# A macaron block on one core: order of two weight loads, of a root and of two kinds of parts

## The reference

```python
x = x + 0.5 * ffn(layernorm(x))
x = x + mamba2_mixer(layernorm(x))
x = x + 0.5 * ffn(layernorm(x))
```

## Time and profile before

| what | value |
| --- | --- |
| median of 3 runs | 1654.56 us |
| the runs | 1654.16, 1654.56, 1661.31 us |
| the profiled execution: its own time | 1658.09 us |
| its span, first to last instruction | 1656.2 us |
| TensorE (PE) busy | 1621.9 us, 98% of the span |
| VectorE (DVE), ScalarE (ACT), GpSimd (POOL) busy | 1033.3, 626.5, 377.0 us |
| mean granted clock of TensorE | 0.999 |

### The profile page before, as it was taken

One profiled execution on the slowest core, in us unless ns is written; L12 is line 12 of the kernel. 1 busy time (PEld: TensorE's weight loads), 2 busy tenths in 40 slices (PEclk: granted clock), 3 DMA queues, 4 the chain that ended last, 5 costly groups with the idle time before them and its releaser, 6 DMA issues.

```text
span 1656.2 us, 25046 instructions
## 1 busy us (share of the span) xinstructions
PE 1621.9 (98%) x9672; PEld 1311.9 (79%) x9672; DVE 1033.3 (62%) x2022; ACT 626.5 (38%) x934; POOL 377.0 (23%) x298
## 2 busy tenths in 40 slices
PE   6999999989999999999999999999999999999999
PEld 3788788867888778888877888877888877888887
DVE  6444345766676877777786677777675683543333
ACT  4334334454333464333355334256333341122111
POOL 1655662012222212222122122122122121000000
PEclk9999999999999999999999999999999999999999
DMA  9755654744455354444435445545544447556763
GB/s 286 293 190 208 224 196 165 254 167 157 155 157 167 130 176 148 158 161 151 163 119 174 165 150 166 162 135 184 165 155 156 155 128 217 166 178 187 219 199 131
DMA packets 253427, 290.46 MB, mean 175 GB/s; under 512 B 14464, under 2 KB 211200, under 8 KB 244096
## 3 DMA queue, kind: packets, MB, share of 16 engines
q1 hardware_dynamic: 253312, 288.88, 53.4%
HBM read 238.51 MB, written 50.33 MB: 174 GB/s over the span
## 4 chain that ended last, share of the span: by engine, by line
PE 72%; DVE 4%; ACT 2%; issue 1%; DMA 0%; SPq 0%; ACTq 0%; DVEq 0%
PE bank L1184 30%; PE bank L1225 14%; PE bank L1140 12%; PE bank L1253 5%; PE bank L1322 3%; PE bank L1293 2%; PE bank L1309 2%; PE bank L1271 2%; PE bank L1316 1%; PE bank L1281 1%; DVE xT L1740 0%; DVE m_cv L1781 0%; DVE res L1766 0%; PE bank L1168 0%; PE bank L1150 0%
## 5 line engine op out<-in xcount | busy, mean ns | idle before, releaser
L1184 PE MATMUL bank<-fxT,wj 128*128 128x512 f32 x1752 | 415.3, 390 | 1.2 <-DVE xn L1753 1.2
L1184 PEld LDWEIGHTS bank<-fxT,wj 128*128 128x128 f32 x1752 | 328.7, 188 | 70.1 <-DVE xn L1753 1.7
L1225 PE MATMUL bank<-m_wd,m_hb 128*128 128x512 f32 x1128 | 278.8, 393 | 1.9 <-DVE m_hb L1759 1.9
L1225 PEld LDWEIGHTS bank<-m_wd,m_hb 128*128 128x128 f32 x1128 | 209.1, 188 | 47.3 <-issue 5.0
L1535 ACT CAST m_hb<-xn 128x512 fp32r<-128x512 f32 x96 | 59.5, 620 | 455.1 <-DVE xn L1753 455.1
L1140 PE MATMUL bank<-xT,wi 128*128 128x512 f32 x900 | 222.6, 395 | 1.6 <-DVE m_cv L1781 0.5
L1140 PEld LDWEIGHTS bank<-xT,wi 128*128 128x128 f32 x900 | 166.1, 188 | 39.1 <-issue 4.5
L1766 DVE TENSOR_TENSOR res<-bank,res 128x512 f32<-128x512 f32 x192 | 132.5, 690 | 83.4 <-PE bank L1225 81.2
L2084 POOL TENSOR_TENSOR m_L<-m_L,m_GT 128x512 f32<-128x512 f32 x36 | 52.6, 1461 | 436.0 <-ACT m_L L1544 436.0
L1753 DVE SCALAR_TENSOR_TENSOR xn<-bank,sc,xn 128x512 f32<-128x512 f32 x96 | 71.8, 748 | 123.0 <-PE bank L1184 122.9
L1529 ACT ACTIVATE xn<-bank,sc 128x512 f32<-128x512 f32 x96 | 66.1, 688 | 145.8 <-PE bank L1184 140.3
(11 more groups left out here) (222 smaller groups left out, 2312.4 us busy)
## 6 DMA issues: line engine op xcount, KB each, us to landing
wj<-ug_split SPq DMA_DIRECT2D x167, 512.0 KB, 4.2
m_wd<-dn_split SPq DMA_DIRECT2D x48, 1024.0 KB, 4.8
wi<-in_split SPq DMA_DIRECT2D x76, 512.0 KB, 3.3
ug_split<-b_wu SPq DMA_DIRECT2D x8, 2048.0 KB, 14.1
m_wo<-out_split SPq DMA_DIRECT2D x32, 512.0 KB, 4.1
wi<-ug_split SPq DMA_DIRECT2D x25, 512.0 KB, 4.1
in_split<-b_msp SPq DMA_DIRECT2D x20, 512.0 KB, 3.7
raw<-in_wug SPq DMA_DIRECT2D x8, 1024.0 KB, 7.0
```

The costliest lines, as they stand in the source:

```text
L1184: ins = pe.matmul(to[:], w[:, a, k, :], frm[:, b, k, :], start=(k == 0 and i == 0), stop=(k == KH - 1 and i == 2))
L1225: ins = pe.matmul(F[t % 2][:], hb[:, a, j, ck(t)], wd[:, b, j, :], start=(j == 0 and n == 0), stop=(j == 1 and n == 2))
```

## The change

Three places are changed.

- In the second stage SyncE issues `load_up(131)` and `load_up(132)` ahead of `load_down(32)`, where they came right behind it. For items 0 to 2 nothing moves there.
- For the sixth item's statistics VectorE runs the second `next` in block b = 4 and the third with `bias` in b = 5; both and `bias` were in b = 4. On ScalarE the four `beside_row`s of b = 5 move behind `hidden_high(37, 1)` and `silu(38, 0)`.
- In the first stage ScalarE casts the parts for the next unit's turns (`high_half`) ahead of the unit's two mixer blocks (`high_blocks`), and GpSimd subtracts in the same order (`low_half` ahead of `low_block`).

No instruction is added or removed.

```diff
--- before.py
+++ after.py
@@ -441,11 +441,11 @@
                 for g in range(2):
                     if g and c + 2 < NC:
                         butterflies(c + 2, True)
+                    for key in halves_of(2 * c + g + 1):
+                        low_half(key)
                     if c:
                         low_block(4 * (c - 1) + 2 * g)
                         low_block(4 * (c - 1) + 2 * g + 1)
-                    for key in halves_of(2 * c + g + 1):
-                        low_half(key)
 
         @block.tensor
         def _(pe):
@@ -688,9 +688,9 @@
                     hidden_high(n, j)
                 for key in keys[3]:
                     turn(key)
-                high_blocks(n)
                 for key in halves_of(n + 1):
                     high_half(key)
+                high_blocks(n)
             silu(UNITS - 1, 0)
             silu(UNITS - 1, 1)
             high_blocks(UNITS - 1)
@@ -1086,6 +1086,9 @@
                         load_out(last_pair(q, b) + 1)
                     if not end:
                         load_up(4 * at + 7)
+                if q == BATCH - 1:
+                    load_up(4 * NC * BATCH + 3)
+                    load_up(4 * NC * BATCH + 4)
                 if other:
                     load_down(NC * (q + 1))
                 if more:
@@ -1094,10 +1097,8 @@
                     keep(q + 1)
                     heads(q + 1, 0)
                     load_in(m0 + 2 * NB + 6)
-                if mix:
+                if more:
                     load_up(4 * NC * (q + 1) + 3)
-                if q == BATCH - 1:
-                    load_up(4 * NC * BATCH + 4)
                 if q >= 2:
                     g = beside(q)
                     for t in range(TPG):
@@ -1713,12 +1714,12 @@
                 if at == NC * BATCH:
                     square(q - 1, NB - 1)
                 silu(at, 1)
+                hidden_high(at, 1)
+                if at < NC * ITEMS - 1:
+                    silu(at + 1, 0)
                 if q == BATCH and b == 5:
                     for t in range(TPG):
                         beside_row(q + 1, t)
-                hidden_high(at, 1)
-                if at < NC * ITEMS - 1:
-                    silu(at + 1, 0)
                 if q == BATCH and b == 6:
                     for t in range(TPG):
                         beside_turn(q + 1, t)
@@ -2047,10 +2048,9 @@
                     norm(q - 1)
                 if q == BATCH and b == 2:
                     ending(q - 1)
-                if q == BATCH and b in (3, 4):
+                if q == BATCH and b in (3, 4, 5):
                     next(other)
-                if q == BATCH and b == 4:
-                    next(other)
+                if q == BATCH and b == 5:
                     bias(1, s_fs)
                 hidden(at, 1)
                 if pair >= 0:
```

## The result

The changed kernel takes 1651.62 us in the median of 20 runs (1648.65 to 1656.31), the kernel before 1656.89 us, also in 20 runs (1654.03 to 1661.31), the three of the table above among them. The ratio is 0.9967 with a 95% interval of 0.9960 to 0.9974, so the change gains 5.5 us of 1656.9, between 4.3 and 6.6. The forecast was 4.83 us, and 1649.7 us against a median of before that stood at 1654.56 then. The profiled execution has a span of 1652.4 us, 3.8 less than before.

The account below looks back on a forecast made before the run. TensorE's stream was taken to bound the kernel, so only its waits count: 2.58 + 1.65 + 0.60 = 4.83 us, taking the median from 1654.56 to 1649.7 us, range 1645.5 to 1657.

Parts of the forecast that it names:

- The bound: Whole kernel: TensorE busy 1621.9 us of a 1656.2 us span; only its waits, 34.3 us idle in all, can be saved.
- The rival that nothing arrives at the end: Whole kernel: a later point is not bound by TensorE's stream, so no gain, 1654.6 us; chance 0.07.
- First stage, 2.58 us: First stage: with parts ahead of blocks, four late pairs of units return to 35.78 us; gain 2.58 us, bounds 0 and 2.6.
- The count of the block loads' delay: First stage: loads into `mraw` land 3.7 us later, ScalarE's `silu` comes 1.3 us late, cost to TensorE 0.
- The cover: First stage: the bank is free at about 207.2, TensorE's third turn needs it at 209.8, so 2.6 us are left.
- the first stage's count: First stage: fetched weights come at 192.3 instead of 188.6, butterflies end at 197.1, GpSimd's next parts covered by about 1 us.
- Fifth item, 1.65 us: Second stage, fifth item: loads ahead of the down load remove the wait before `up1(32)`; gain 1.65 us, bounds 0 and 1.7.
- Sixth item, 0.60 us: Second stage, blocks 4 and 5: root over three blocks removes `down`'s wait for VectorE's hidden value; gain 0.60 us, bounds 0.47 and 0.7.
- The step on ScalarE's rows: Sixth item: four rows, 2.92 us, move behind `silu(38, 0)`; unmoved they would stand before a cast that `down(37)` needs.
- The sum: Whole kernel: 2.58 + 1.65 + 0.60 = 4.83 us, median from 1654.56 to 1649.7 us, 0.29% less.
- One of its own signs of being wrong: Whole kernel: prediction wrong if the three gains are there and the span is not 4 to 5 us shorter.
- The rival on the slower side: First stage: late block loads hold ScalarE, TensorE waits 3.7 us in each of four units, 1667.1 us; chance 0.04.

## Why the prediction was right

- **The bound.** TensorE's stream sets the time from the first stage to the end; its busy time stayed within 0.2 us (1624.4 us in the second profile of the changed kernel, where the clock fell for longer) and what was removed are waits. The rival that nothing arrives at the end is refuted by the ratio.
- **First stage, 2.58 us.** 2.54 in the changed kernel's profile, 2.55 in the profile and 2.2 (0.7 to 3.5) by time with this part alone. The count of the block loads' delay held: 3.7 us forecast, 3.80 in unit 9; `silu` 1.3 us late, 1.21 measured. ScalarE's waits for `mraw` in units 4, 6, 8 and 10 are 4.13, 5.15, 4.83 and 3.90 us, some 4 forecast. The cover was given as 2.6 us and is some 2.9, since two turns stand between the products that were counted.
- **What the first stage's count left out.** The fetched weights came later than worked out: from unit 8's begin to the first butterfly 5.6 us before and 10.5 us now (183.08 and 181.29 are those begins), 4.9 and not 3.7 us. The load was issued 3.7 us later and took 8.1 us to landing where it took 7.0. The prediction asked only whether GpSimd would be in time with the parts. It did not ask what VectorE would do beside the butterflies, and VectorE lost 2.2 us there (3.63 for 1.46). That 0.9 us of cover were left on this path was luck: in the run with added work on GpSimd they were used up.
- **Fifth item, 1.65 us.** 1.7 us from `down` to `down` in the run with the loads alone; 1.3 us (0.0 to 2.8) by time. No wait came up behind it.
- **Sixth item, 0.60 us.** 0.65 us in the profiles, too small for the time. The step on ScalarE's rows was wrong in what it would cost not to move them: the prediction had them "in front of a cast that `down(37)` needs", and the run with the rows kept shows no wait. They are in front of it and end just in time. The whole gain is that of the root.
- **The sum.** 4.83 us forecast; 5.5 (4.3 to 6.6) measured. The three parts alone measured 2.2, 1.3 and 0.5 us, together 4.0, with intervals of more than a microsecond each way: they add up as far as this can tell. The absolute 1649.7 was 1.9 us low: the median of before rose by 2.3 us, from 1654.56 over 3 runs to 1656.89 over 20, and the two medians are 5.3 us apart and not 4.8.
- **One of its own signs of being wrong came true.** It said that with the three gains there the span must be 4 to 5 us shorter; it is 3.8 us shorter. The profile shows what came between: 1.2 us for the clock at the start of the second stage and 0.9 us for the load of the cumulative sums, neither in the sum nor in a place that the change touches.
- **The rival on the slower side** was a real mechanism that the changed kernel stays clear of: with some 4 us more delay TensorE waits where the prediction said, and also on VectorE's path, and all of the gain is gone (ratio 0.9998). With GpSimd's half of the edit alone the time is 23 us worse.

That each DMA engine takes the descriptors of a ring in order was taken from the Trainium skill ("DMA: Bandwidth & Descriptors", "Queues, rings and completion order"); that a delay therefore passes through in full was the prediction's conclusion. The trace agrees for the loads into `mraw`: issued 4.0 us later in unit 8 (6.10 us behind its begin for 2.10), cast 3.80 us later in unit 9. The fetched weights were issued 3.7 us later and arrived 4.9 us later, so there the delay was more than full.

What is left open: why the clock falls at the start of the second stage in some executions and not in others, and whether the part of the ratio beyond 4.8 us is more than the interval's width. The clock may have a share in it. Of the changed kernel's 20 runs 12 have a mean clock of 0.999 or more, of the 65 runs of before that stand beside the experiments 14. Between runs of the same mean clock the medians are 3.9 us (0.998), 4.7 us (0.996) and 6.5 us (0.999) apart, with 3 to 11 runs of the changed kernel in each and not run beside one another, so this does not settle it.

## What to carry to other kernels

When two engines pass pieces on to each other in a written order, change the order on both or on neither: ScalarE's half of this edit alone cost 6 us (one run; 8.7 us in its profile's first stage), GpSimd's half 23 us, and the whole gained 2.5. Before a long transfer is let slip, work out who waits in order behind its consumer and how far off the real deadline is; here 3.8 us of delay were free and 4 us more were not. Ask also what the late engine will then run beside: the path that came nearest to a wait here was not that of the late load, but VectorE's work next to GpSimd's. Gains of one or two microseconds in 1650 are seen in the distance between two fixed matmuls of one profile, to some hundredths where the clock does not fall, long before runs can tell them.

## What was not expected of the hardware

In the kernel's second stage TensorE stands still for 0.6 and 1.6 us between short products. Between the same two matmuls there, in kernels with the same order at that place, the stretch took 26.99 to 27.04 us in four profiles with the full 2.4 GHz throughout (before among them), 28.23 to 29.05 us in three in which 3.4 us of it were at 1.2 GHz, and 30.38 to 30.56 us in three in which 10.2 us were. Two executions of the changed kernel gave 28.23 and 30.56 us. A difference of up to 3.5 us between two profiles is thus no difference between two kernels, and it may be part of what the runs of one kernel scatter by: of 65 runs of before, the 5 with a mean clock of 1.000 have a median of 1654.60 us and the 13 with 0.996 one of 1658.54. The fall was seen only behind idle time; with GpSimd's half alone, behind its longer waits, it was seen four times more in the first stage, with ScalarE's half once.

VectorE's subtraction of one hidden low part took 0.68 or 0.69 us in the kernel before from 68 us of the span on, where GpSimd was idle beside it or worked for 0.1 us of it. In the changed kernel those in unit 8 took 1.93 and 1.77 us, with GpSimd's butterflies and parts running beside them throughout, and with the added work 2.66 and 2.88 us. GpSimd's first part behind took 1.74 us there for 1.31 in unit 7. That the two engines hold each other up is read from these rows; no run was made to show it.
